# The order of the key tile and the value tile within an attention step on TensorE

## What is computed

```
lat = layer_norm(latents, ln_lat_g, ln_lat_b)
ctx = layer_norm(context, ln_ctx_g, ln_ctx_b)
q = lat @ Wq                      # 16 heads of 64
k, v = split(ctx @ Wkv)           # 16 heads of 64 each, 2048 rows a batch
k = apply_rope(k, cos, sin)
attn = clip(einsum('bhnd,bhsd->bhns', q, k) * 64 ** -0.5, -11.0, 11.0)
out = einsum('bhns,bhsd->bhnd', softmax(attn), v)
x = x + out @ Wo + bo
```

## Time and profile before

| | us |
|---|---|
| median of 3 runs | 1477.66 (1475.86 to 1479.48) |
| profiled execution, its own time | 1473.42 |
| its span, from the first to the last instruction | 1471.7 |
| TensorE busy | 1379.6 (94%) |
| DVE, ACT, POOL busy | 848.8, 795.0, 844.3 |
| mean granted TensorE clock | 0.978 |

### The profile page before, as it was taken

One profiled execution on the slowest core, in us unless ns is written; L12 is line 12 of the kernel. 1 busy time (PEld: TensorE's weight loads), 2 busy tenths in 40 slices (PEclk: granted clock), 3 DMA queues, 4 the chain that ended last, 5 costly groups with the idle time before them and its releaser, 6 DMA issues. The chain is left out here.

```text
span 1471.7 us, 25168 instructions
## 1 busy us (share of the span) xinstructions
PE 1379.6 (94%) x8732; PEld 1128.4 (77%) x8732; DVE 848.8 (58%) x1414; ACT 795.0 (54%) x1227; POOL 844.3 (57%) x727
## 2 busy tenths in 40 slices
PE   4899999999999999999999999999997779999993
PEld 2578888888788888878888888888885366866662
DVE  7356665666556566656665666565553456665552
ACT  2346566656566666656566656666554312445560
POOL 3467677767677777767677767777664243200002
PEclk9999999999999999999999999999999889899997
DMA  6667666766667766657666766677665560569983
GB/s 207 207 113 131 123 116 114 129 117 136 120 108 130 122 123 112 134 108 125 124 117 126 115 133 119 122 118 120 131 102 119 192 237 0 194 244 360 348 332 107
DMA packets 115236, 218.44 MB, mean 148 GB/s; under 512 B 13328, under 2 KB 49168, under 8 KB 108944
## 3 DMA queue, kind: packets, MB, share of 16 engines
q1 hardware_dynamic: 111648, 208.48, 63.1%
q0 software_dynamic: 1280, 4.20, 0.9%
q10 hardware_dynamic: 2160, 3.93, 0.7%
HBM read 132.67 MB, written 16.78 MB: 102 GB/s over the span
## 5 line engine op out<-in xcount | busy, mean ns | idle before, releaser
L576 POOL TENSOR_TENSOR p_parts<-probs,p_parts 128x512 fp32r<-128x512 f32 x256 | 340.2, 1349 | 249.1 <-ACT p_parts L625 249.0
L625 ACT ACTIVATE p_parts<-probs 128x512 fp32r<-128x512 f32 x256 | 148.0, 626 | 243.8 <-PE banks L859 235.0
L727 DVE TENSOR_TENSOR probs<-banks,probs 128x1024 f32<-128x1024 f32 x128 | 156.7, 1224 | 158.6 <-ACT probs L631 158.6
L670 ACT ACTIVATE probs<-probs 128x1024 f32<-128x1024 f32 x128 | 136.0, 1063 | 142.3 <-POOL probs L583 141.9
L811 PE MATMUL banks<-wv_hi,x_hi 128*128 128x512 f32 x512 | 207.6, 405 | 3.9 <-PEq L169 3.9
L812 PE MATMUL banks<-wv_lo,x_hi 128*128 128x512 f32 x512 | 202.0, 394 | 0.0
L826 PE MATMUL banks<-x_hi,wk_hi 128*128 128x512 f32 x512 | 201.9, 394 | 0.0
L813 PE MATMUL banks<-wv_hi,x_lo 128*128 128x512 f32 x512 | 201.0, 393 | 0.0
L828 PE MATMUL banks<-x_hi,wk_lo 128*128 128x512 f32 x512 | 199.6, 390 | 0.0
L827 PE MATMUL banks<-x_lo,wk_hi 128*128 128x512 f32 x512 | 199.3, 389 | 0.0
L859 PE MATMUL banks<-p_parts,v_hi 128*65 128x128 f32 x1024 | 191.1, 223 | 0.0
(11 more groups left out here) (255 smaller groups left out, 2686.4 us busy)
## 6 DMA issues: line engine op xcount, KB each, us to landing
queries<-q_scratch SPq DMA_DIRECT2D x256, 128.0 KB, 6.0
keys<-wo_room SPq DMA_DIRECT2D x128, 256.0 KB, 5.5
keys<-turned_odd SPq DMA_DIRECT2D x128, 256.0 KB, 5.6
row_room<-in_ctx SPq DMA_DIRECT2D x64, 256.0 KB, 6.2
wo_room<-in_down SPq DMA_DIRECT2D x10, 1024.0 KB, 6.8
wo<-in_gate SPq DMA_DIRECT2D x8, 1024.0 KB
gate_raw<-in_up SPq DMA_DIRECT2D x8, 1024.0 KB, 10.1
up_raw<-in_gate SPq DMA_DIRECT2D x7, 1024.0 KB, 8.3
```

The costliest lines, as they stand in the source:

```text
L576: nc.gpsimd.tensor_tensor(p_parts[:, 1, j, :], probs[:, pair % 2, j, :], p_parts[:, 0, j, :].bitcast(F32), ALU.subtract).then_inc(p_lo_rea ...
L727: nc.vector.tensor_tensor(mine, ps_s[:, :, :, 0, :].rearrange("p j i n -> p (j i) n"), mine, ALU.add).then_inc(s_taken, 1)
```

## The change

In TensorE's `step`, the call of `keys_of` moves from behind `turn_sums` to the place ahead of the first half of the values. All steps have the new order. No other engine's program is touched.

```diff
                 score(b, t - SCORE_LAG)
                 if ending:
                     fill(t, 0)
+                keys_of(b, t)
                 values(b, t, (0, 1))
                 tile = row_tile_of(b, t)
                 if tile is not None:
...
                     transpose_row_tile(nc, rows, pe, b * ROWS_OF_BATCH + tile, tile % ROW_TILES)
                 values(b, t, (2, 3))
                 turn_sums(b, t - VALUE_LAG - 1)
-                keys_of(b, t)
                 weigh(b, t - VALUE_LAG)
```

## The result

The changed kernel takes 1508.83 us (median of 4 runs, 1507.74 to 1512.01) against 1478.23 us of the kernel before (4 runs): ratio 1.0203, 95% interval 1.0173 to 1.0232, so 30.6 us slower. The forecast was 1508.6 in a range of 1492 to 1527. The profiled execution is the slowest of the four, 1512.01 us with a span of 1510.3, and that of the kernel before (1473.42 us) is faster than all four of its runs; the difference of the two spans, 38.6 us, is therefore more than that of the medians.

A forecast was written before the change was run, and what follows sets the result against it. TensorE (PE) was taken to bound the attention loop, waiting for nobody. Waits of 22.5 us in plain odd steps and 11.4 in turning steps, less 3.0 at start-up, gave +30.9 us on the median 1477.66: 1508.6 us, range 1492 to 1527.

The forecast's parts named there:

- both places: PE would wait at `weigh` for ACT's x_full in odd steps, and at the keys for DVE's turned key tile.
- both counts (57 and 12): 57 waits at `weigh` in odd steps from step 5, and 12 at the keys next to turned sums.
- 45 plain odd steps, `full_ready`: `weigh` in odd steps without turned sums: waits for x_full, 0.50 us each, 22.5 us in all.
- 12 turning pairs: Steps that turn the sums: waits of 0.40 us at `weigh` and 0.55 at the keys, 11.4 us in all.
- start-up, to the end of step 5: Before the pipeline is full: four PE waits, for normalised rows and the first keys, would close, -3.0 us.
- start and restart: At `weigh` behind x_full: 0.05 us from producer's end to PE's start, plus 0.07 for restarting behind a wait.
- the bounds: For the wait at `weigh`: 0.3 to 0.8 us a step, the upper with register instructions and a second wait.
- the rule that I took from the Trainium skill: At `weigh`: weight loads cannot be pulled ahead behind an open wait, leaving 0.136 us bare; the sum kept 0.07.
- The even turning steps: Even steps with turned sums: the turned key tile comes in time for the following keys, by 0.18 us.
- all four should close: Start-up: PE's waits of 0.55, 0.63 and 1.10 us for rows and 0.76 for the first keys vanish.
- The exponential behind x_full: ACT in odd steps: the exponential ends later, still half a microsecond before the next ACT work; nothing lost.

The follow-up runs named there:

- e10: The changed kernel with the hardware loop over three batches written out; 1490.00 us, ratio 1.0076 to the kernel before.
- e11: The changed kernel, loop kept, with `weigh`'s wait for `full_ready` moved behind its other waits onto the first matmul; 1503.49 us, ratio 1.0163 to the kernel before.
- e1: The changed kernel with the four transposes of odd steps moved behind the key tile, ahead of all values; 1484.29 us, ratio 1.0036 to the kernel before.
- e4: The changed kernel with the four transposes moved behind all values, directly ahead of the turned sums and `weigh`; 1585.02 us, ratio 1.0718 to the kernel before.
- e5: The changed kernel with only two of ACT's four x_full instructions, so its output is not the reference's; 1482.92 us, ratio 1.0023 to the kernel before.
- e2: The changed kernel with transposes and turned sums both moved behind the key tile, ahead of all values; 1474.77 us, ratio 0.9967 to the kernel before.
- e6: The kernel before with the key tile moved only ahead of the second half of the values, behind the transposes; 1475.98 us, ratio 0.9971 to the kernel before.
- e8: The kernel before with the hardware loop over three batches written out; 1470.25 us, ratio 0.9930 to the kernel before.

## Why the prediction was right, point by point

The direction, both places, both counts (57 and 12) and the time hold. Two names differ: the profile puts the first waits down to "issue" instead of L663, and the second to L699, the last of the two multiplications, instead of L698. The sizes, from the two traces:

| term | forecast | measured |
|---|---|---|
| 45 plain odd steps, `full_ready` | 45 x 0.50 = 22.5 | 17.7 (33 in the loop) + 3.0 (7 behind it) + 2.2 (4 beside the branch, taken at 0.55) = 22.9; step 5 is in the start-up |
| 12 turning pairs | 11.4 | 4.2 (odd) + 2.8 (even) + 1.4 (plain even behind the last) = 8.4 |
| start-up, to the end of step 5 | -3.0 | 43.28 - 44.93 = -1.6; -2.6 in e10 and e11 |
| branch of the loop | not in the sum | +4.6 in these two executions |

- *`full_ready`, 0.50.* Right to 0.05: the lateness of x_full is 708.26 - 707.95 = 0.31, the start behind it 0.20, the slower beginning of `weigh` 0.04. I had the lateness at 0.32 to 0.39 and the start and restart at 0.12. The missing part is the register instruction behind the wait, which I had put in the bounds as 0.1 to 0.15 and left out of the value; it costs 0.08 (e11) to 0.12 (e10). By the rule that I took from the Trainium skill (TensorE: Matmul & The Clock Gate, section on the architectural detail of the array) the restart would have been 0.136 instead of 0.07. The trace agrees with the rule, but not with the price: behind the wait the load starts at 708.45, 0.01 ahead of its matmul, where without a wait such a load ran 0.23 ahead of its matmul in the kernel before (667.88 against 668.11); but that matmul did not wait for the load's 0.13 us to pass. Without register instructions the start behind ACT and the restart are 0.10 in e10 and the 0.04 of `weigh`, together 0.14 against my 0.12, so the rows were nearer than a whole load on top of 0.05.
- *Turning steps, 0.95 a pair.* The mechanism holds, the term was too large: it measured 0.70. The wait at `weigh` is 8.94 - 8.51 (e1) = 0.43 against 0.40, the one at the keys 8.51 - 8.05 (e4) = 0.46 against 0.55. What I missed is that the two turned sums are cheaper at their new place: ahead of the keys they lengthen an even step by 8.16 - 7.92 = 0.24, ahead of `weigh` by 8.05 - 7.91 = 0.14, about 0.1 less in each of 24 steps. The even turning steps fitted, as said: their following keys don't wait.
- *Start-up, -3.0.* The step "all four should close" failed in one of the four. The three waits for rows did close. The wait for the first keys stayed, 0.63 us against the 0.76 of the earlier trace rows. I had looked at when the key tile is made, not at the engine behind it. In the changed kernel ACT rounds the first keys (L650) at 75.09. DVE had them ready at 72.23 + 0.69 = 72.92, but ACT had x_full (L663), its rounding (L148) and the copy of value tile 1 (L641) ahead of them; value tile 1 itself was out at 74.05 by the modelled end of its last matmul. In e5, where x_full is half as long, the keys are rounded at 74.47 and PE does not wait for them:

```profile
72.71 1.51 ACT L663 ACTIVATE row_room<-banks,ctx_b,ctx_g 128x128 f32<-128x128 f32 x4 [3.94 <-PE banks L133]
74.09 0.64 ACT L148 ACTIVATE x_hi<-row_room 128x512 fp32r<-128x512 f32 x1
74.61 0.61 ACT L641 ACTIVATE v_hi<-banks 128x512 fp32r<-128x512 f32 x1
75.09 1.17 ACT L650 ACTIVATE wo_room<-wo_room 128x512 fp32r<-128x512 f32 x2
```

The -1.6 of the table says less than it seems to. In the changed kernel's trace the granted clock was 0.50 to 0.52 from 59 to 65 us, in the one before 0.62 and 0.53 from 58 to 62 and 1.00 from there. e10 and e11 have the same order on PE at the start and a shorter stretch at half clock (0.58 and 0.56 from 58 to 62 in e10), and take 42.29 us, 2.6 less than before. With the new order the wait at `weigh` of step 5 stands in this stretch as well, some 0.4 us (8.75 us from scores to scores against 8.36 in e1), which the forecast counts in its first term. So the term itself was between -2.0 and -3.0. The sum of the waits was also not all that was to be had: in e1 and e2, where all four are closed, the start-up takes 41.08 and 41.34 us, 3.6 to 3.9 less.

- *The exponential behind x_full* cost nothing, as said: it starts at 708.14, straight behind x_full, and the next ACT work waits for `weigh` anyway.
- *The branch.* Not foreseen. PE's two holes there have 3.0 and 3.4 us before and 3.8 and 4.1 after, and after both of them PE ran at half clock for a while (granted clock 0.50 from 394 to 398 and from 673 to 679 us), before behind the second only (0.50 from 653 to 655; 1.00 from 384 on). The six steps around the two branches take 58.3 us before and 65.1 after, 62.9 without their four waits at `weigh`; e1, e2, e5 and e6 have 60.7 to 63.7. e6 has the values first and takes 61.1, so the execution profiled before was the cheapest of all at the branch, and much of the 4.6 is likely chance. Whether the holes themselves grow because PE's sequencer, held by `full_ready`, reaches the branch later is a guess; e1 and e2 have 3.5 and 4.0 as their longest without that wait, which speaks against it. It stays open.

The sum of the measured terms without the branch is 22.9 + 8.4 - 1.6 = 29.7 us, with it 34.3, against 30.9 forecast and 30.6 between the medians. (The same terms from e8 and e10 sum to 23.6, and their medians differ by 19.8.) The spans of the two traces differ by 38.6: 1.1 more lie ahead of the first matmul of the attention and 3.3 behind step 117, 1.7 of them in the half clock at L883 that is shown below. So 1508.6 against 1508.8 is nearer than the terms deserve, and in that part luck: the turning steps were 3.0 too high, the start-up 1.4 too low in this execution, the branch was left out, and single executions differ by more than all of these.

## What to carry to other kernels

When one engine is the bound and never waits, moving its own work cannot gain more than the few waits it has; ask for each of its waits how many microseconds of its work lie between what it sends out and what it needs back. Here the moved block was the cover of somebody else's round trip, and each microsecond of cover below the round trip was paid in full. If a block must move, move the start of the round trips with it: transposes and sums ahead of the values made key-first as fast as value-first, and writing the loop out gained more (e8, 9.5 us) than any order did (e2, 4.1 us).

## What the runs showed of the hardware

- **A register instruction between a wait and the matmul costs about 0.1 us** when that wait ends last: 8.94 in the loop, 8.82 with constants, 8.86 with the wait on the matmul; from ACT's end to PE's start 0.20, 0.10 and 0.15. `k_turned`, whose register instruction stands ahead of its wait, starts PE 0.05 us after DVE's end (618.23 to 618.28). In the changed kernel the profile also names no producer for such a wait ("issue", 56 of 57), in e11 it does (57 of 57). That is not the register instruction's doing alone: e10, with constants, has "issue" too.
- **The branch of a hardware loop** left PE idle for 2.9 to 5.0 us each time it was taken back (16 holes in eight kernels); the loop over three batches written out gained 9.5 us between the medians (0.9930), and 8.9 us in the six steps around the branches of the two traces.
- **Half clock behind a hole is not certain.** Behind the same wait of 2.18 us for L616 at the end of the attention, the same eight matmuls took 3.67 us in one execution (granted clock 1.00) and 5.37 in another (0.50 from 1172 to 1174 us). Written out it was the other way round, 5.37 in e8 and 3.67 in e10, so it is not the order that decides. Before:

```profile
1135.45 3.67 PE L883 MATMUL banks<-wo,wo_room 128*128 128x512 f32 x8 [2.18 <-ACT wo_room L616]
```

After:

```profile
1170.37 5.37 PE L883 MATMUL banks<-wo,wo_room 128*128 128x512 f32 x8 [2.18 <-ACT wo_room L616]
```

Runs of one kernel here lie up to 15 us apart. Such differences of 1.7 us at one place, and more behind the branch, may be part of the reason; only one execution of each kernel has a trace, so this is not shown.
